# Scan products in sixteen 32x32 tiles and four banks, with the state kept in SBUF and updated by VectorE

## Chip, core and metric

The kernel runs on one core of a Trainium2 chip. The metric is the device time of one execution in microseconds (us), the median of several runs.

## What is computed

One block of a transformer on x of shape (2, 4096, 512), in fp32. Only the scan in its attention part is touched by the change:

```python
k, v = x @ Wk.T, x @ Wv.T                  # 16 heads of 32; k is rotated by position (cos/sin)
W = eye(32) per batch and head             # the state
for each chunk of 16 tokens (256 chunks):
    z    = kc @ W
    grad = kc.T @ ((z - vc) * 2/(16*32))
    W    = W - grad
out = layernorm(z of all chunks) * gamma + beta
x1  = layernorm(x + out @ Wo.T)
y   = down(silu(gate(x1)) * up(x1))        # 512 -> 1408 -> 512, ternary weights with scales
result = layernorm(x1 + y)
```

The chunks depend on one another: 256 steps, each of which reads the state that the step before it left.

## The kernel before

The work goes in ticks. Tick t takes tokens 128t to 128t+127 of both batches, and each tick works on several such tiles of tokens at once, at different depths: it projects k and v of tile t, and of tile t+1 for batch 0 (`project_k`, `project_v`, `rotate`), runs the eight scan steps of tile t-1 (sc), normalises z of tile t-2 and projects it with Wo (`project_o`, `add_o`), and does the feed-forward of tiles t-2 and t-3 (`gate_up`, `down`), of which the last normalisation belongs to tile t-4. A tick has 16 slots (`SLOTS`). Every engine runs its own written-out list of slots, in order, and waits on semaphores; there is no scheduler. What stands in a slot, and in which order inside it, is the order on that engine's queue.

Scan step i takes two slots. In the even slot 2i TensorE makes z (`scan_z`, line 698: 16 fp32 products of 64 columns on tiles of 64x32, each of them two records in the trace), VectorE subtracts v from it (`scan_err`, line 925: four instructions, one for each quarter of the partitions, which leave the other half of every `err` row block at zero), and ScalarE copies z out of PSUM into `v_rows` for storing (`save_z`, line 519). In the odd slot 2i+1 TensorE adds the products of k and err to the state in PSUM (`scan_state`, line 713: 8 products of 128 columns on tiles of 64x32, which accumulate for the whole kernel), and ScalarE copies the state from PSUM to SBUF with the factor -STEP (`keep_state`, `copy_state`, line 510: four instructions), where the next `scan_z` reads it.

Between the scan's products TensorE has full-size work. After the state products of slot 13 it does `down` (line 751, four products) and then the first nine products of `project_v` for batch 0 of the next tile (line 725). These wait for `k_mul`, which VectorE's `rotate` raises (lines 909 and 914), since both projections use the one PSUM bank `work`: rotate reads k from it, and then v may overwrite it. `rotate(t + 1, 0)` is VectorE's first item in slot 13.

```python
dve.wait_ge(k_projected, 2 * n + b + 1)      # rotate: three operations, then k_mul is at 6n + 3b + 3
pe.wait_ge(k_mul, 6 * n + 3 * b + 3)         # project_v
```

In slots 0, 2, 8 and 10 ScalarE's `save_z` stands behind `gate` (line 534), which waits for that slot's `gate_up` on TensorE. Ticks 3 to 30 all have this form (28 of them). In tick 1 and most of tick 2 there is no feed-forward work, and ticks 31 and 32 have no projection of a new tile.

## Time and profile before

| | us |
|---|---|
| median of 3 runs | 2057.38 |
| lowest, highest | 2052.96, 2057.82 |
| the profiled execution | 2071.61 |
| its span, first to last instruction | 2069.7 |
| mean granted TensorE clock in it | 0.965 of full |

The page gives the busy time of every engine; the windows view splits it by stage; the lines view groups instructions by line, with the mean of one and the idle time of the engine just before them; the timeline shows instructions in order of time. "issue" as a releaser is idle time for which the profile shows no wait. PE is TensorE's products, PEld its weight loads, DVE is VectorE, ACT ScalarE, POOL GpSimd.

### The profile page before, as it was taken

Reading aid. Unit: us, or ns where it says so; the run is one execution under the profiler, and the core shown is the slowest. Engines: PE = TensorE matmul, PEld = TensorE weight load, DVE = VectorE, ACT = ScalarE, POOL = GpSimd, SP = SyncE. Lnnn points to the kernel's source line nnn. Section 1 sums busy time; section 2 is a strip of 40 time slices with the busy share of each in tenths; the row PEclk is TensorE's granted clock in tenths of the full one; section 3 lists DMA queues with packets and bytes.
Section 4 is the critical chain, followed back from the end, with each engine's and each line's share of the span. In section 5 each row is a group of like instructions: output and inputs, shape, how many; then the busy total and the mean of one; then the engine's idle time right before and its main releaser. Section 6 shows DMA issues by size and latency. Waiting matters only on the chain.

```text
span 2069.7 us, 53846 instructions
## 1 busy us (share of the span) xinstructions
PE 1869.2 (90%) x21656; PEld 1460.7 (71%) x21656; DVE 1300.4 (63%) x2878; ACT 914.4 (44%) x2258; POOL 641.1 (31%) x778
## 2 busy tenths in 40 slices
PE   3235999999999999999999999999999999999887
PEld 2123777777777777777777777777777777777765
DVE  2247676667666766676666667666676676666642
ACT  1122544444444444444444444444444444444422
POOL 1001233332333333323323333233333333333222
PEclk8677999999999999999999999999999999999999
DMA  5574444454555444544544445445444454444320
GB/s 188 191 221 142 135 143 143 140 153 128 148 157 153 139 137 140 153 132 145 157 150 130 147 141 150 134 145 155 144 140 146 142 149 130 149 146 147 93 78 27
DMA packets 314194, 294.02 MB, mean 142 GB/s; under 512 B 42968, under 2 KB 264408, under 8 KB 313944
## 3 DMA queue, kind: packets, MB, share of 16 engines
q1 hardware_dynamic: 302048, 272.21, 44.2%
q10 hardware_dynamic: 11896, 18.35, 2.7%
q8 instruction: 173, 2.83, 0.6%
q14 instruction: 77, 0.63, 0.1%
HBM read 156.19 MB, written 142.87 MB: 144 GB/s over the span
## 4 chain that ended last, share of the span: by engine, by line
PE 47%; DVE 24%; DMA 11%; issue 7%; SPq 4%; ACT 3%; POOL 2%; ACTq 1%; DVEq 0%; POOLq 0%
PE work L725 18%; PE gu_acc L739 16%; DVE err L925 9%; PE down_acc L751 8%; DMA landed<-zT_scr 5%; DMA zT_scr<-turned 4%; DVE hid L932 3%; DVE turned L864 3%; PE z_acc L698 2%; DVE stats L845 2%; DVE x_tok L859 2%; PE state_acc L713 2%; POOL rstd L431 2%; SPq L307 2%; SPq L261 2%
## 5 line engine op out<-in xcount | busy, mean ns | idle before, releaser
L453 POOL TENSOR_TENSOR hid_lo<-hid,hid_hi 128x256 fp32r<-128x256 f32 x352 | 261.8, 744 | 905.1 <-ACT hid_hi L544 905.1
L925 DVE TENSOR_TENSOR err<-z_acc,v_rows 32x256 f32<-32x256 f32 x1024 | 429.1, 419 | 113.8 <-PE z_acc L698 87.8
L510 ACT ACTIVATE state<-state_acc 32x256 f32<-32x256 f32 x1028 | 384.5, 374 | 76.3 <-PE state_acc L713 57.0
L739 PE MATMUL gu_acc<-x_hi,gw 128*128 128x256 f32 x1408 | 386.3, 307 | 34.0 <-DVE hid L932 30.9
L534 ACT ACTIVATE hid<-gu_acc,gate_scale 128x256 f32<-128x256 f32 x352 | 166.7, 474 | 413.0 <-PE gu_acc L739 412.2
L739 PE MATMUL gu_acc<-x_lo,gw 128*128 128x256 f32 x1408 | 348.1, 280 | 0.0
L739 PE MATMUL gu_acc<-x_hi,uw 128*128 128x256 f32 x1408 | 347.5, 280 | 0.0
L739 PE MATMUL gu_acc<-x_lo,uw 128*128 128x256 f32 x1408 | 346.9, 279 | 0.0
L739 PEld LDWEIGHTS gu_acc<-x_hi,gw 128*128 128x128 f32 x1408 | 265.3, 188 | 98.9 <-DVE hid L932 74.9
L932 DVE SCALAR_TENSOR_TENSOR hid<-gu_acc,up_scale,hid 128x256 f32<-128x256 f32 x352 | 168.8, 479 | 262.2 <-ACT hid L534 258.4
L751 PE MATMUL down_acc<-dw,hid_hi 128*128 128x512 f32 x704 | 281.8, 400 | 1.0 <-POOL hid_lo L453 1.0
L751 PE MATMUL down_acc<-dw,hid_lo 128*128 128x512 f32 x704 | 278.7, 396 | 0.0
L739 PEld LDWEIGHTS gu_acc<-x_lo,gw 128*128 128x128 f32 x1408 | 266.0, 189 | 0.1
L739 PEld LDWEIGHTS gu_acc<-x_hi,uw 128*128 128x128 f32 x1408 | 265.0, 188 | 0.0
L739 PEld LDWEIGHTS gu_acc<-x_lo,uw 128*128 128x128 f32 x1408 | 264.8, 188 | 0.0
L519 ACT ACTIVATE v_rows<-z_acc 128x256 f32<-128x256 f32 x256 | 97.6, 381 | 342.9 <-DVE err L925 342.9
L725 PE MATMUL work<-wv,fm 128*128 128x512 f32 x744 | 196.9, 407 | 56.9 <-DVE k_sin L914 56.9
L544 ACT ACTIVATE hid_hi<-hid 128x256 fp32r<-128x256 f32 x352 | 147.1, 418 | 175.7 <-DVE hid L932 174.8
L725 PE MATMUL work<-wo,fm 128*128 128x512 f32 x768 | 200.2, 411 | 25.9 <-DVE fm L946 24.5
L725 PE MATMUL work<-wk,fm 128*128 128x512 f32 x756 | 201.9, 416 | 10.6 <-DVE fm L956 10.6
L725 PEld LDWEIGHTS work<-wv,fm 128*128 128x128 f32 x744 | 137.8, 192 | 89.9 <-DVE k_sin L914 57.9
L725 PEld LDWEIGHTS work<-wo,fm 128*128 128x128 f32 x768 | 144.2, 194 | 62.1 <-DVE fm L946 28.1
(74 smaller groups left out, 2083.9 us busy)
## 6 DMA issues: line engine op xcount, KB each, us to landing
x_fm<-xT SPq DMA_DIRECT2D x64, 256.0 KB, 3.5
k_scr<-k_tok SPq DMA_DIRECT2D x32, 512.0 KB, 3.9
k_rows<-k_scr SPq DMA_DIRECT2D x512, 32.0 KB, 2.1
v_rows<-v_scr SPq DMA_DIRECT2D x512, 32.0 KB, 2.1
z_scr<-v_rows SPq DMA_DIRECT2D x32, 512.0 KB, 3.2
z_tok<-z_scr SPq DMA_DIRECT2D x512, 32.0 KB, 1.8
x_tok<-x SPq DMA_DIRECT2D x32, 512.0 KB, 3.8
zT_scr<-turned SPq DMA_DIRECT2D x128, 128.0 KB, 3.1
```

The source lines that it names most:

```text
L261: sp.dma_start(place[:, i0:i0 + NS // 2, :], scr[b, i0 * MB:i0 * MB + P // 2, hg * P:(hg + 1) * P] .rearrange("(i t) c -> t i c", t=MB)).t ...
L453: pool.tensor_tensor(hid_lo[m % RING][:], hid[m % 2][:], hid_hi[m % RING][:].bitcast(F32), ALU.subtract).then_inc(hid_lo_ready, 1)
L510: act.activation(state[q, :, e].rearrange("p (r g) e -> p r g e", r=2), state_acc[q, :, 0:P].rearrange("p r (g e) -> p r g e", e=HEAD), AC ...
L519: act.activation(v_rows[:, i].rearrange("p a (r c) -> p a r c", r=2), z_acc[:, :, 0:P].rearrange("p r (a c) -> p a r c", a=2), ACT.Copy).t ...
L534: act.activation(hid[m % 2][:], gu_acc[:, 0:TOK], ACT.Silu, scale=gate_scale[:, m:m + 1]).then_inc(silu_done, 1)
L544: act.activation(hid_hi[m % RING][:], hid[m % 2][:], ACT.Copy).then_inc(hid_hi_ready, 1)
L725: mm = pe.matmul(acc[:], lhsT=fm[p_x][:, c, b, :], rhs=w[p_w][:, c, :], start=(c == 0 and k == 0), stop=(c == NC - 1 and k == 2))
L739: mm = pe.matmul(gu_acc[:, k * TOK:(k + 1) * TOK], lhsT=w[:, c, m * P:(m + 1) * P].bitcast(dt), rhs=part[:, c].bitcast(dt), start=(c == 0 ...
L751: mm = pe.matmul(down_acc[b][:], lhsT=part[m % RING][:, b * P:(b + 1) * P].bitcast(dt), rhs=dw[:, m, :].bitcast(dt), start=(m == 0 and par ...
L864: dve.transpose(turned[:, :, b * NC:(b + 1) * NC, :], src[:, b, :].rearrange("p (c h d) -> p h c d", c=NC, h=HQ)).then_inc(done, 1)
L925: dve.tensor_tensor(err[q, g:g + 2, :, :].rearrange("p a (r h) e -> p a r (h e)", r=2), z_acc[q, :, 0:P].rearrange("p r (a c) -> p a r c", ...
L932: dve.scalar_tensor_tensor(hid[m % 2][:], gu_acc[:, TOK:2 * TOK], up_scale[:, m:m + 1], hid[m % 2][:], ALU.mult, ALU.mult).then_inc(hid_re ...
```

## The change

The four PSUM banks of state and z become one tensor `scan_acc` of four banks. z stays in columns 0 to 127 of banks 2 and 3. The product of k and err no longer accumulates in PSUM: it is 16 products of 64 columns on tiles of 32x32, row tile j into columns 128 to 191 of bank j (`step_acc`). `err` holds no zero halves any more, and is written by one instruction over 128 partitions. The state lives in SBUF; VectorE adds the step to it with two instructions (`step_state`), whose scalar column `half_step` is -STEP on the partitions that belong to the half and 0 on the others. ScalarE's `copy_state` and `keep_state` are gone. `scan_z` no longer waits for `z_saved`; `scan_state` waits for it ahead of row tile 2. The state's starting value is loaded by a DMA and `begin_state` is gone.

```diff
-        err = sb("err", [P, NG // 2, HQ, HEAD])
+        err = sb("err", [P, 2, HQ, HEAD])
+        half_step = sb("half_step", [P, 2])
...
-        state_acc = bank_pair("state_acc")
-        z_acc = bank_pair("z_acc")
+        scan_acc = ctx.enter_context(nc.psum_tensor("scan_acc", [P, NG // 2, 512], F32))
+        z_acc = scan_acc[:, 2:4, 0:P]
+        step_acc = scan_acc[:, :, P:P + 2 * HEAD]
...
-            sp.dma_start(eye_rep, ident_rep.rearrange("p (g e) -> p g e", g=NG)).then_inc(small_in, 16)
+            sp.dma_start(state[:], begin.rearrange("p (g e) -> p g e", g=NG)).then_inc(small_in, 16)
...
             def save_z(n, i):
-                act.wait_ge(err_ready, 4 * NS * n + 4 * i + 4)
+                act.wait_ge(err_ready, NS * n + i + 1)
...
-                    if within(sc) and s % 2 == 1:
-                        keep_state(sc, s // 2)
...
             def scan_z(n, i):
-                pe.wait_ge(state_ready, 4 * NS * n + 4 * i + 4)
                 if i >= 1 or n >= 1:
-                    pe.wait_ge(z_saved, NS * n + i)
+                    pe.wait_ge(state_ready, 2 * (NS * n + i))
...
             def scan_state(n, i):
-                pe.wait_ge(err_ready, 4 * NS * n + 4 * i + 4)
-                for r in range(2):
-                    k = slice(r * P // 2, (r + 1) * P // 2)
+                pe.wait_ge(err_ready, NS * n + i + 1)
+                for j in range(NG // 2):
+                    k = slice(j * HEAD, (j + 1) * HEAD)
+                    if j == 2:
+                        pe.wait_ge(z_saved, NS * n + i + 1)
                     for h in range(HQ):
                         q = slice(h * HEAD, (h + 1) * HEAD)
-                        mm = pe.matmul(state_acc[q, r, 0:P], lhsT=k_rows[k, i, q], rhs=err[k, :, h, :],
-                                       start=False, stop=False, skip_group_check=True,
-                                       tile_position=(r * P // 2, h * HEAD))
-                        if r:
+                        mm = pe.matmul(step_acc[q, j, :], lhsT=k_rows[k, i, q], rhs=err[k, :, h, :], start=True,
+                                       stop=True, skip_group_check=True, tile_position=(j * HEAD, h * HEAD))
+                        if j == NG // 2 - 1:
                             mm.then_inc(state_added, 1)
...
             def scan_err(n, i):
-                for j in range(NG // 2):
-                    q = slice(j * HEAD, (j + 1) * HEAD)
-                    g = j % 2 * 2
-                    dve.wait_ge(z_done, 4 * NS * n + 4 * i + j + 1)
-                    dve.tensor_tensor(err[q, g:g + 2, :, :].rearrange("p a (r h) e -> p a r (h e)", r=2),
-                                      z_acc[q, :, 0:P].rearrange("p r (a c) -> p a r c", a=2),
-                                      v_rows[q, i].rearrange("p a (r c) -> p a r c", r=2),
-                                      ALU.subtract).then_inc(err_ready, 1)
+                dve.wait_ge(z_done, 4 * NS * n + 4 * i + 4)
+                dve.tensor_tensor(err[:].rearrange("p a (r h) e -> p a r (h e)", r=2),
+                                  z_acc.rearrange("p r (a c) -> p a r c", a=2),
+                                  v_rows[:, i].rearrange("p a (r c) -> p a r c", r=2),
+                                  ALU.subtract).then_inc(err_ready, 1)
+
+            def step_state(n, i):
+
+                dve.wait_ge(state_added, 4 * NS * n + 4 * i + 4)
+                for e in range(2):
+                    part = state[:, :, e * HEAD:(e + 1) * HEAD].rearrange("p (j o) e -> p j o e", o=2)
+                    dve.scalar_tensor_tensor(part, step_acc.rearrange("p j (o e) -> p j o e", o=2),
+                                             half_step[:, e:e + 1], part, ALU.mult, ALU.add).then_inc(state_ready, 1)
...
                 for s in range(SLOTS):
+                    if within(sc) and s % 2 == 1:
+                        step_state(sc, s // 2)
                     if within(o) and s in (7, 8):
                         add_o(o, s - 7)
```

On VectorE's queue, slots 12 to 14 of a steady tick stood so before (`x_lo` is the low part of x1, `x_tok<-down_acc` the scaling of the feed-forward's output):

```order
L925 TENSOR_TENSOR err<-z_acc,v_rows 32x256 [waits z_done] x4
L961 TENSOR_TENSOR x_lo<-landed,x_hi 128x4x128 [waits x1_hi_ready]
L909 TENSOR_TENSOR k_tok<-work,rot 128x512 [waits k_turned,k_stored,v_stored,rot_in0,k_projected]
L914 TENSOR_TENSOR k_sin<-work,rot 128x16x16 x2
L961 TENSOR_TENSOR x_lo<-landed,x_hi 128x4x128 [waits x1_hi_ready]
L942 TENSOR_TENSOR x_tok<-down_acc,down_scale 128x512 [waits down_done,x1_ready]
```

and now so (line numbers are those of the changed file):

```order
L890 TENSOR_TENSOR err<-scan_acc,v_rows 128x256 [waits z_done]
L934 TENSOR_TENSOR x_lo<-landed,x_hi 128x4x128 [waits x1_hi_ready]
L900 SCALAR_TENSOR_TENSOR state<-scan_acc,half_step,state 128x8x32 [waits state_added]
L900 SCALAR_TENSOR_TENSOR state<-scan_acc,half_step,state 128x8x32
L877 TENSOR_TENSOR k_tok<-work,rot 128x512 [waits k_turned,k_stored,v_stored,rot_in0,k_projected]
L882 TENSOR_TENSOR k_sin<-work,rot 128x16x16 x2
L934 TENSOR_TENSOR x_lo<-landed,x_hi 128x4x128 [waits x1_hi_ready]
```

Four instructions have become one, and two new ones, which wait for TensorE's `state_added`, stand ahead of the three of `rotate`.

On TensorE's queue, slot 13 and the start of slot 14 stood so before:

```order
L713 MATMUL state_acc<-err,k_rows 32x128 [waits err_ready]
L713 MATMUL state_acc<-err,k_rows 32x128 x7
L751 MATMUL down_acc<-dw,hid_hi 128x512 [waits hid_lo_ready]
L751 MATMUL down_acc<-dw,hid_lo 128x512
L751 MATMUL down_acc<-dw,hid_hi 128x512
L751 MATMUL down_acc<-dw,hid_lo 128x512
L725 MATMUL work<-wv,fm 128x512 [waits k_mul]
L725 MATMUL work<-wv,fm 128x512 x8
L698 MATMUL z_acc<-state,k_cols 32x64 [waits z_saved,state_ready]
```

and now so:

```order
L684 MATMUL scan_acc<-err,k_rows 32x64 [waits err_ready]
L684 MATMUL scan_acc<-err,k_rows 32x64 x7
L684 MATMUL scan_acc<-err,k_rows 32x64 [waits z_saved]
L684 MATMUL scan_acc<-err,k_rows 32x64 x7
L721 MATMUL down_acc<-dw,hid_hi 128x512 [waits hid_lo_ready]
L721 MATMUL down_acc<-dw,hid_lo 128x512
L721 MATMUL down_acc<-dw,hid_hi 128x512
L721 MATMUL down_acc<-dw,hid_lo 128x512
L695 MATMUL work<-wv,fm 128x512 [waits k_mul]
L695 MATMUL work<-wv,fm 128x512 x8
L667 MATMUL scan_acc<-state,k_cols 32x64 [waits state_ready]
```

The order is the same, with eight more products in the state block and a second wait in its middle; the nine products of `project_v` still wait for `k_mul`.

## Rows read from the trace of the kernel before

**Rows 1.** Page, part 1: busy time (share of the span) and instructions.
```profile
PE 1869.2 (90%) x21656; PEld 1460.7 (71%) x21656; DVE 1300.4 (63%) x2878; ACT 914.4 (44%) x2258; POOL 641.1 (31%) x778
```

**Rows 2.** Windows: stretch, length, busy of PE, PEld, DVE, ACT, POOL, clock, DMA.
```profile
89.75:208.00 118.25, 59.15 (x887) 38.20 (x887) 68.17 (x123) 35.71 (x89) 11.73 (x15) 0.74 0.64 191
208.00:1900.00 1692.00, 1647.55 (x19376) 1293.50 (x19376) 1135.62 (x2545) 808.23 (x2007) 568.93 (x686) 1.00 0.49 144
1900.00:1980.00 80.00, 67.84 (x876) 53.78 (x875) 49.19 (x112) 38.05 (x97) 24.29 (x31) 0.96 0.33 98
```

**Rows 3.** Page, part 5: busy, mean ns of one, idle before.
```profile
L925 DVE TENSOR_TENSOR err<-z_acc,v_rows 32x256 f32<-32x256 f32 x1024 | 429.1, 419 | 113.8 <-PE z_acc L698 87.8
L510 ACT ACTIVATE state<-state_acc 32x256 f32<-32x256 f32 x1028 | 384.5, 374 | 76.3 <-PE state_acc L713 57.0
L932 DVE SCALAR_TENSOR_TENSOR hid<-gu_acc,up_scale,hid 128x256 f32<-128x256 f32 x352 | 168.8, 479 | 262.2 <-ACT hid L534 258.4
```

**Rows 4.** Timeline, slot 13 of tick 16: start, duration, engine, [idle before it].
```profile
1026.32 0.69 DVE L909 TENSOR_TENSOR k_tok<-work,rot 128x512 f32<-128x512 f32 x1
1026.63 0.18 PEld L713 LDWEIGHTS state_acc<-err,k_rows 64*32 64x32 f32 x16 [0.36 <-issue]
...
1026.93 0.74 DVE L914 TENSOR_TENSOR k_sin<-work,rot 128x256 f32<-128x256 f32 x2
...
1027.01 0.50 PE L751 MATMUL down_acc<-dw,hid_hi 128*128 128x512 f32 x1
...
1027.26 1.58 ACT L510 ACTIVATE state<-state_acc 32x256 f32<-32x256 f32 x4 [1.18 <-PE state_acc L713]
...
1028.04 2.26 PE L725 MATMUL work<-wv,fm 128*128 128x512 f32 x9
```

**Rows 5.** Timeline, the z block of slot 12, same tick.
```profile
1022.32 0.29 PEld L698 LDWEIGHTS z_acc<-state,k_cols 64*32 64x32 f32 x32 [0.36 <-issue]
...
1022.70 2.63 PEld L725 LDWEIGHTS work<-wk,fm 128*128 128x128 f32 x12
```

**Rows 6.** Lines by form, TensorE's two scan blocks.
```profile
L698 PE MATMUL z_acc<-state,k_cols 64*32 64x64 f32 x8192 | 118.5, 225 | 20.0 <-ACT state L510 20.0
L713 PE MATMUL state_acc<-err,k_rows 64*32 64x128 f32 x4096 | 116.6, 285 | 42.0 <-DVE err L925 42.0
```

**Rows 7.** Timeline, slot 8 of the same tick: ScalarE's save of z, then TensorE.
```profile
1010.75 0.38 ACT L519 ACTIVATE v_rows<-z_acc 128x256 f32<-128x256 f32 x1
...
1011.20 0.45 PE L713 MATMUL state_acc<-err,k_rows 64*32 64x128 f32 x16
```

**Rows 8.** Timeline, project_o after a wait, in two ticks; the clock after the first.
```profile
764.26 4.61 PE L725 MATMUL work<-wo,fm 128*128 128x512 f32 x12 [1.97 <-DVE fm L946]
...
1060.12 3.07 PE L725 MATMUL work<-wo,fm 128*128 128x512 f32 x12 [2.38 <-DVE fm L946]
...
764.30:769.00 4.70, 4.70 (x28) 3.31 (x28) 3.94 (x9) 1.00 (x3) 0.73 (x1) 0.64 0.12 42
```

**Rows 9.** Waits: engine, line, waited for, us in total, times, longest.
```profile
PEld gu_acc L739 <- DVE hid L932: 74.9, 173, 1.8
```

**Rows 10.** Timeline of ticks 1 and 2, before the feed-forward has started.
```profile
107.30 1.77 DVE L925 TENSOR_TENSOR err<-z_acc,v_rows 32x256 f32<-32x256 f32 x4 [4.77 <-PE z_acc L698]
...
109.13 0.45 PE L713 MATMUL state_acc<-err,k_rows 64*32 64x128 f32 x16 [1.90 <-DVE err L925]
...
111.44 0.68 PE L698 MATMUL z_acc<-state,k_cols 64*32 64x64 f32 x32 [1.85 <-ACT state L510]
...
149.87 1.29 DVE L845 BATCH_NORM_STATS2 stats<-z_tok 128x6 f32<-128x512 f32 x2 [13.51 <-DMA z_tok<-z_scr]
```

**Rows 11.** Timeline of ticks 31 and 32: first, longest and last scan waits.
```profile
1912.48 0.45 PE L713 MATMUL state_acc<-err,k_rows 64*32 64x128 f32 x16 [0.78 <-DVE err L925]
...
1929.45 0.46 PE L698 MATMUL z_acc<-state,k_cols 64*32 64x64 f32 x32 [2.05 <-ACT state L510]
...
1972.67 0.46 PE L698 MATMUL z_acc<-state,k_cols 64*32 64x64 f32 x32 [1.33 <-ACT state L510]
```

More of the change, by code:

```diff
@@ L39 @@
 HALF_UNITS = {1: (0, 2), 2: (2, NC)}
+ZEROED = 3
+SMALL = 8
 LN_EPS = 1e-5
@@ L46, in within, with build @@
     return 0 <= n < NT
-def build(nc, xT, x, wkT, wvT, woT, gamma, beta, gwT, uwT, dwT, gs, us, ds_row, rope, ident, ident_rep, out):
+def build(nc, xT, x, wkT, wvT, woT, gamma, beta, gwT, uwT, dwT, gs, us, ds_row, rope, ident, begin, halves, out):
     with ExitStack() as ctx:
@@ L266, in load_k_half0 @@
                 sp.wait_ge(k_stored, 16 * (n + 1))
-                if n == 0:
-                    sp.wait_ge(state_begun, 2 * HQ)
-                else:
+                if n >= 1:
                     sp.wait_ge(state_added, 4 * NS * (n - 1) + 2 * NS)
@@ L423, in _ @@
         def _(pool):
-            for buf in (v_rows, k_cols, err, state):
+            for buf in (v_rows, k_cols):
                 pool.memset(buf[:], 0.0).then_inc(zeroed, 1)
             pool.memset(neg_half[:], -0.5).then_inc(zeroed, 1)
-            pool.wait_ge(zeroed, 5)
+            pool.wait_ge(zeroed, ZEROED)
             def inverse_root(norm, n):
@@ L504, in _ @@
         def _(act):
-            def copy_state():
-                for h in range(HQ):
-                    q = slice(h * HEAD, (h + 1) * HEAD)
-                    e = slice(h % 2 * HEAD, (h % 2 + 1) * HEAD)
-                    act.activation(state[q, :, e].rearrange("p (r g) e -> p r g e", r=2),
-                                   state_acc[q, :, 0:P].rearrange("p r (g e) -> p r g e", e=HEAD),
-                                   ACT.Copy, scale=-STEP).then_inc(state_ready, 1)
             def high_part(w, stage, c):
@@ L666, in _ @@
         def _(pe):
-            def begin_state():
-                pe.wait_ge(small_in, 16 * 7)
-                pe.wait_ge(zeroed, 5)
-                for r in range(2):
-                    for h in range(HQ):
-                        q = slice(h * HEAD, (h + 1) * HEAD)
-                        pe.matmul(state_acc[q, r, 0:P], lhsT=eye[:, q],
-                                  rhs=eye_rep[:, r * NG // 2:(r + 1) * NG // 2, :], start=True, stop=False,
-                                  skip_group_check=True, tile_position=(0, h * HEAD)).then_inc(state_begun, 1)
             def find_bias():
@@ L689, in scan_z @@
                     pe.wait_ge(k_cols_ready, 4 * n + (2 if i == 0 else 4))
-                pe.wait_ge(state_ready, 4 * NS * n + 4 * i + 4)
                 if i >= 1 or n >= 1:
-                    pe.wait_ge(z_saved, NS * n + i)
+                    pe.wait_ge(state_ready, 2 * (NS * n + i))
+                else:
+                    pe.wait_ge(small_in, 16 * SMALL)
                 for odd in range(2):
@@ L798, in tick @@
                         gate_up(f1, EARLY_GU[s], ffn_dt)
-                    if t == 0 and s == 0:
-                        begin_state()
                     if within(t) and t >= EARLY_TICKS and s == 1:
@@ L1074 @@
     eye = np.eye(P, dtype=np.float32)
-    eye_rep = np.zeros((P, NG, HEAD), np.float32)
+    begin = np.zeros((P, NG, 2 * HEAD), np.float32)
+    halves = np.zeros((P, 2), np.float32)
     for p in range(P):
-        eye_rep[p, :, p % HEAD] = -1.0 / STEP
+        begin[p, :, p % (2 * HEAD)] = 1.0
+        halves[p, p // HEAD % 2] = -STEP
     arrays = {
@@ L1084 @@
         "ds_row": np.broadcast_to(np.asarray(L0_ffn_down_s), (P, DM)),
-        "rope": rope_table(), "ident": eye, "ident_rep": eye_rep.reshape(P, NG * HEAD),
+        "rope": rope_table(), "ident": eye, "begin": begin.reshape(P, NG * 2 * HEAD),
+        "halves": halves,
     }
```

23 lines of the change are left out of this document (6 added, 17 removed).

## The prediction

> **What bounds the kernel.** I read the page's busy times first: TensorE has products under way for 90% of the span, VectorE 63%, ScalarE 44% [rows 1]. A share over the whole span mixes stages, so the windows come next [rows 2]. From 208 to 1900 us TensorE is busy 1647.6 of 1692 us at full clock, so there the order on its queue is the time. From 89.75 to 208 us it is busy for half of 118 us, at 0.74 of its clock, and at the end, 1900 to 1980, for 67.8 of 80 us. In those two stretches something else ends the waits, and the scan is a candidate.
>
> In the steady ticks the scan's own waits are nearly absent: TensorE waited 42.0 us for `err` and 20.0 us for the state copy in the whole run [rows 6], and the timeline puts most of that before 208 and after 1900. The scan chain is hidden behind `gate_up`, `down` and the projections. So making it shorter is worth nothing there, and what counts is whether the change makes TensorE wait in a place where it does not wait now.
>
> **Part by part, against the profiled execution's 2071.6 us.**
>
> *ScalarE* loses 1028 copies of 374 ns, 384.5 us [rows 3]. In the steady ticks nobody waits for them, so this is worth about nothing.
>
> *VectorE.* Before, `err` was 1024 instructions of 419 ns, 429 us [rows 3]. The length of an instruction goes with the elements of a partition, not with the number of partitions, so one over 128 partitions also takes some 0.42 us: 256 of them are 107 us, 322 us less. Added are 512 instructions of 256 elements, of the same kind as the scaling of hid, 479 ns [rows 3]: +245 us. VectorE becomes emptier, by 77 us, but its queue gets a new kind of wait: in each odd slot it now stands still until TensorE has done that slot's state block.
>
> *Slot 13, the term that decides.* In tick 16 `rotate` starts at 1026.32 and is done at 1027.67, while TensorE does its state block and four products of `down`; TensorE then starts `project_v` at 1028.04 without a wait [rows 4]. The slack is under 0.4 us. In the new order the two state updates stand in front of `rotate`. They cannot start before the state block is done, and the row that shows when that is seen by another engine is ScalarE's copy, which had waited 1.18 us for it and starts at 1027.26 [rows 4]. On VectorE the next instruction starts some 0.08 us before the one ahead has ended (1026.32 + 0.69 against 1026.93), so the pair takes 2 x 0.40 = 0.80 us from `rotate`'s view: it starts at 1028.06 and ends at 1029.41 instead of 1027.67. TensorE's first product moves from 1028.04 to about 1029.45, and the first product after a pause is 0.1 us longer (0.50 against 0.40) [rows 4]: 1.5 us. Behind the waiting VectorE stand low_x1 and the scaling of y, both needed only later; behind the waiting TensorE stands the whole tick, and no later wait in the tick is on anything that is not started from this same queue, so the 1.5 us are not given back. Ticks 3 to 30 are 28 ticks: **+42 us**. Ends: a pair of 0.70 to 0.96 us gives 1.4 to 1.7 us, +39 to +47.
>
> *The clock after such a stall.* The steady trace has six waits of 1.57 to 2.38 us ahead of `project_o`. After three of them the granted clock fell (0.64 in the 4.7 us behind the first, so for a part of it at the 1.2 GHz level) and the twelve products took up to 4.61 us instead of 3.07; after the other three, the longest among them, it did not [rows 8]. The new stall is at the short end and has four full products between it and the state block. I take one tick in four: 7 x 1.5 = **+10 us**; ends 0 and 28 x 1.5 = +42.
>
> *The state block itself.* Before, 16 records of 128 columns on 8 tiles; now 32 records of 64 columns on 16 tiles. The nearest row is the z block, 32 records of 64 columns on 8 tiles. From its first weight load to the next full-size one it takes 0.38 us (1022.32 to 1022.70) [rows 5], and the state block takes the same 0.38 (1026.63 to 1027.01), both after 0.36 us of "issue" [rows 4, 5]. Busy time per block is equal too, 118.5/256 and 116.6/256 us [rows 6]. So: **0**. Ends: 0.08 us less a block, since a record is 225 instead of 285 ns [rows 6] (-20 us in 256 blocks), and 0.04 more (+10).
>
> The second wait, for `z_saved`, could stop the block in its middle. In slots 0, 2, 8 and 10 the save stands behind `gate`; in slot 8 it ran from 1010.75 to 1011.13, and the block starts at 1011.20 [rows 7]. It just fits, and the other slots have more room: 0, within the +10.
>
> By the Trainium skill, TensorE: Matmul & The Clock Gate, section Measured speedup vs the span model, a packed group takes one product's duration plus some 4 ns for each further one. With a record of 225 ns and 31 more that is 0.35 us of busy time against 0.46, or an estimated 28 us less in 256 blocks, and a total near 2061; the z block, also 32 records, does not follow it, with 0.46.
>
> *Waits for hid.* TensorE's weight loads waited 74.9 us in 173 cases for the scaling of hid [rows 9], part of it because VectorE was at `err` or ScalarE at a save or copy. With `err` 1.3 us shorter I take 0.25 us a tick: **-7 us**; ends 0 and -12.
>
> *The start.* In tick 1 a step is limited by the chain: 1.77 us of `err`, 1.90 us waited by the state products, 1.85 us waited by the next z [rows 10]. The new chain is shorter by 1.35 us in `err` and 0.7 us in the copy (1.58 against 0.88), less some 0.4 us for the save of z, about 1.6 us a step where no projection stands between. That holds in about half of tick 1's eight steps. But then VectorE waits 13.5 us for a DMA that brings z_tok [rows 10], in a stretch where the DMA queues carry 191 GB/s [rows 2]; this wait starts earlier, and need not end as much earlier. In tick 2 VectorE itself is the busy one (68.2 of 118 us), and z of the second step has to wait for a state update that stands behind that DMA wait. I take **-8 us**, ends 0 and -14. The setup that goes (`begin_state` and a first copy) is covered by transfers. Tick 2 also has the stall of slot 13: **+1**.
>
> *The end.* Ticks 31 and 32 have six scan waits of 0.78 to 2.05 us [rows 11], 8.2 us together, and no `rotate`. The shorter chain takes most: **-6 us**, ends 0 and -8.
>
> Sum: +42 + 10 + 0 - 7 - 8 + 1 - 6 = **+32 us**, 2103.6 against the profiled 2071.6. The median of the runs is 14.2 us (0.7%) below that execution, so I put the difference on it: 2057.4 + 32 = **2089 us**. With the middling ends of the terms this case runs from 2064 to 2112.
>
> **Rivals.**
>
> *A. The clock falls at most of the stalls.* Same stall, but its cost is 3.0 instead of 1.5 us in nearly every tick. For it: three of six waits of this length did so. Against: the longest did not, and dense work stands around the new one. +32 + 32 = 2121 us. Chance 0.10.
>
> *B. Faster: the state block is cheaper.* Place: the eight state blocks of a tick. If sixteen tiles really work side by side, the block shrinks to one weight load and its drain, some 0.2 of 0.38 us, and 256 blocks give back 46 us: 2089 - 46 = 2043 us. It decides from 0.13 us a block, where the 32 us are paid back; above it the kernel gets faster. Against: the z block has the same count of records and shows no such thing. Chance 0.08.
>
> *C. The small gains cancel the stall.* No change of clock, 0.04 us less a block (-10), start -14, end -8, hid -12: 43 - 44 = -1, or 2056 us. Each end is possible, all together are not likely. Chance 0.07.
>
> The forecast case, slower with a clock that falls now and then, has 0.75. About 0.3% is what a measurement of this kernel can tell from no change. Slower is the forecast and A, 0.85; the same is C, 0.07; faster is B, 0.08. The range 2062 to 2118 takes in the forecast's ends and part of A, and leaves out B, C and the rest of A.
>
> **What would show it.** Right, if the changed profile has: TensorE waiting some 28 times about 1.4 us ahead of `project_v` (first nine products), released by the k_sin instructions of `rotate`; in each such tick `rotate` directly behind two state updates of 0.4 to 0.5 us; `err` at 256 x 0.42 us; ScalarE's busy time down by 384 us without effect; steady ticks some 1.5 us longer; and 0.38 us from the state block's first weight load to the next full-size one. Wrong, if `project_v` follows `down` without a wait, if the state block is under 0.25 us or over 0.5, if TensorE waits in the middle of it for `z_saved`, or if the clock row shows falls in most ticks. The largest doubt is the clock; the next the start, where DMA and scan take turns.

## The result and the profile after

| | before | after |
|---|---|---|
| median of 6 runs each, same chip, us | 2055.45 | 2068.68 |
| lowest, highest | 2049.06, 2058.63 | 2064.87, 2071.99 |
| the profiled execution | 2071.61 | 2071.99 |
| its span | 2069.7 | 2070.0 |
| mean granted TensorE clock in it | 0.965 | 0.969 |

The ratio is 1.0066, 95% interval 1.0047 to 1.0085: 13 us slower. The direction and the range held; of the 32 us forecast, 13 came. The two profiled executions are equally long, so their difference is not the change's price: the one of before lies some 16 us above the median in the table, the one of after 3 us. They serve to see each part.

Page of the changed kernel, part 1:

```profile
PE 1865.3 (90%) x25736; PEld 1479.9 (71%) x25736; DVE 1176.0 (57%) x2622; ACT 543.8 (26%) x1230; POOL 647.0 (31%) x776
```

Its lines by form (busy, mean ns of one, idle before):

```profile
L900 DVE SCALAR_TENSOR_TENSOR state<-scan_acc,half_step,state 128x256 f32<-128x256 f32 x512 | 223.1, 476 | 221.3 <-PE scan_acc L684 217.3
L890 DVE TENSOR_TENSOR err<-scan_acc,v_rows 128x256 f32<-128x256 f32 x256 | 107.4, 419 | 113.0 <-PE scan_acc L667 101.3 <-DMA v_rows<-v_scr 11.5
L684 PE MATMUL scan_acc<-err,k_rows 32*32 32x64 f32 x8192 | 104.5, 228 | 18.2 <-DVE err L890 18.0
```

`err` over 128 partitions takes the 419 ns that it took over 32 [rows 3], the updates 476 ns. ScalarE lost 371 us of 914 [rows 1], for which TensorE had waited 20.0 us [rows 6], at start and end.

Timeline of slot 13 of tick 16 after, which answers to [rows 4]:

```profile
1028.27 0.23 PEld L684 LDWEIGHTS scan_acc<-err,k_rows 32*32 32x32 f32 x32 [0.37 <-issue]
...
1028.59 0.19 PEld L721 LDWEIGHTS down_acc<-dw,hid_hi 128*128 128x128 f32 x1
...
1028.93 0.88 DVE L900 SCALAR_TENSOR_TENSOR state<-scan_acc,half_step,state 128x256 f32<-128x256 f32 x2 [2.21 <-PE scan_acc L684]
...
1029.72 0.68 DVE L877 TENSOR_TENSOR k_tok<-work,rot 128x512 f32<-128x512 f32 x1
1030.32 0.74 DVE L882 TENSOR_TENSOR k_sin<-work,rot 128x256 f32<-128x256 f32 x2
...
1031.12 2.36 PE L695 MATMUL work<-wv,fm 128*128 128x512 f32 x9 [1.33 <-DVE k_sin L882]
```

VectorE waited 2.21 us for the state block, did both updates, then `rotate`; TensorE stood 1.33 us. Two more things can be read: the state block now takes 0.32 us from its first weight load to the next full-size one (1028.27 to 1028.59), not 0.38, and no wait stands in its middle (in the whole run 1.1 us in 5 cases).

Waits of the whole run after (engine, line, waited for: us in total, times, longest):

```profile
PE work L695 <- DVE k_sin L882: 96.6, 31, 54.5
...
PE scan_acc L667 <- DVE state L900: 18.4, 9, 7.1
PE scan_acc L684 <- DVE err L890: 18.0, 9, 6.3
PE work L695 <- DVE fm L919: 10.4, 11, 3.4
...
PEld gu_acc L709 <- DVE hid L905: 46.0, 77, 1.8
```

Before, the first of these was 56.9 us in 3 cases: 28 stalls have come, as forecast. But two others shrank. The weight loads' waits for hid went from 74.9 in 173 cases [rows 9] to 46.0 in 77; most of that was hidden behind products under way, for the products' own waits for hid went only from 30.9 to 26.6. And the waits of TensorE for `fm`, ahead of `project_o`, went from 24.5 us in 25 cases to 10.4 in 11, of which the steady ticks hold 2.3 us in 6; the three falls of the clock behind such waits [rows 8] are gone as well. The windows of after (compare [rows 2]) show the clock at full in the steady part, where three short falls were too little to show in before's 1.00, and at the end, where before had 0.96:

```profile
89.75:208.00 118.25, 68.24 (x1189) 46.82 (x1189) 61.37 (x110) 15.93 (x33) 13.31 (x17) 0.74 0.64 193
208.00:1900.00 1692.00, 1631.13 (x22867) 1300.13 (x22866) 1019.81 (x2303) 473.53 (x1080) 573.16 (x682) 1.00 0.48 144
1900.00:1980.00 80.00, 71.25 (x1148) 57.25 (x1148) 46.80 (x112) 22.66 (x53) 25.55 (x33) 1.00 0.35 107
```

### The profile page after: what moved, and what is told of

It reads as the page before. It is cut to its first block, busy times and chain, and to the rows that moved or that the text cites. A ratio compares the mean times of both kernels' runs of the same rounds, so it can differ in the third digit from the quotient of the medians.

```text
span 2070.0 us, 60526 instructions
## 1 busy us (share of the span) xinstructions
PE 1865.3 (90%) x25736; PEld 1479.9 (71%) x25736; DVE 1176.0 (57%) x2622; ACT 543.8 (26%) x1230; POOL 647.0 (31%) x776
## 4 chain that ended last, share of the span: by engine, by line
PE 71%; DVE 10%; DMA 6%; issue 6%; ACT 2%; SPq 2%; ACTq 1%; POOL 1%; DVEq 0%; POOLq 0%
PE gu_acc L709 30%; PE work L695 24%; PE down_acc L721 10%; PE scan_acc L684 4%; PE scan_acc L667 4%; DMA landed<-zT_scr 3%; DVE turned L832 3%; DVE state L900 2%; DMA zT_scr<-turned 2%; DVE hid L905 2%; ACT hid L518 1%; ACTq L567 1%; DVE k_sin L882 1%; DVE x_tok L827 1%; SPq L304 1%
## 5 line engine op out<-in xcount | busy, mean ns | idle before, releaser
L709 PE MATMUL gu_acc<-x_hi,gw 128*128 128x256 f32 x1408 | 388.4, 309 | 29.6 <-DVE hid L905 26.6
L709 PE MATMUL gu_acc<-x_hi,uw 128*128 128x256 f32 x1408 | 353.1, 283 | 0.0
L709 PE MATMUL gu_acc<-x_lo,uw 128*128 128x256 f32 x1408 | 351.7, 281 | 0.0
L900 DVE SCALAR_TENSOR_TENSOR state<-scan_acc,half_step,state 128x256 f32<-128x256 f32 x512 | 223.1, 476 | 221.3 <-PE scan_acc L684 217.3
L695 PE MATMUL work<-wo,fm 128*128 128x512 f32 x768 | 198.4, 408 | 12.9 <-DVE fm L919 10.4
L507 ACT ACTIVATE v_rows<-scan_acc 128x256 f32<-128x256 f32 x256 | 97.6, 381 | 358.1 <-DVE err L890 358.1
L695 PEld LDWEIGHTS work<-wk,fm 128*128 128x128 f32 x756 | 141.3, 194 | 46.0 <-DVE fm L929 10.1
```

Source lines behind the costliest of these rows:

```text
L507: act.activation(v_rows[:, i].rearrange("p a (r c) -> p a r c", r=2), z_acc.rearrange("p r (a c) -> p a r c", a=2), ACT.Copy).then_inc(z_s ...
L695: mm = pe.matmul(acc[:], lhsT=fm[p_x][:, c, b, :], rhs=w[p_w][:, c, :], start=(c == 0 and k == 0), stop=(c == NC - 1 and k == 2))
L709: mm = pe.matmul(gu_acc[:, k * TOK:(k + 1) * TOK], lhsT=w[:, c, m * P:(m + 1) * P].bitcast(dt), rhs=part[:, c].bitcast(dt), start=(c == 0 ...
L900: dve.scalar_tensor_tensor(part, step_acc.rearrange("p j (o e) -> p j o e", o=2), half_step[:, e:e + 1], part, ALU.mult, ALU.add).then_inc ...
```

## How the runs are compared

Twelve runs were made in three batches, each on one chip, with the kernel before beside them: "ratio" is the time over that of the kernel before in the same batch. That kernel had medians of 2055 to 2063 us; the changed one had 2068.68 and 2067.27. So a difference between two kernels of different batches is told by ratios and by medians, and where the two disagree by some us, both stand.

From TensorE's timeline I split each profiled execution at the twelve products of `project_v` in slot 4: "start" is the time of the first in tick 3, "tick" the mean of the 28 distances up to tick 31, "shortest" the least of them, "end" the rest of the span. "po" are TensorE's waits of over 0.15 us ahead of `project_o` between 230 and 1840 us, their sum and their number, "falls" the `project_o` in there that took over 4 us for twelve products instead of 3.06.

```
kernel                  ratio   median   start  tick   shortest  end    po        falls
before                  1       2055-63  226.7  59.06  58.03     189.2  20.8, 23  3
after                   1.0066  2068.7   220.5  59.49  59.33     183.7   2.3,  6  0
after again             1.0057  2067.3   212.5  59.52  59.27     185.0   3.8,  7  0
rotate first            0.9802  2022.2   215.1  58.00  57.67     184.3   5.1, 13  0
 + turn later           0.9751  2006.8   214.2  57.39  57.08     184.7   3.8,  7  0
 + err in four          1.0057  2074.4   226.7  59.05  57.93     190.9  17.9, 23  1
err in four             1.0265  2116.9   228.8  60.56  59.53     191.4  14.0, 17  2
 + old tiles            1.0275  2121.9   228.2  60.81  59.91     193.1  13.3, 13  1
four but in step 7      1.0250  2110.6   231.7  60.42  59.49     191.7  12.4, 14  1
four in step 0 alone    1.0104  2085.2   217.3  60.22  59.27     183.5  19.4, 21  2
four but in step 0      1.0217  2108.7   225.4  60.33  59.56     194.4  11.6, 16  1
late save in step 7     1.0060  2069.3   216.5  59.50  59.26     184.8   2.9,  8  0
before + stall          1.0227  2110.9   229.7  60.46  59.68     186.0  16.2, 19  1
before + wait alone     1.0101  2081.7   225.8  59.55  58.76     186.4  16.8, 16  1
```

## The experiments

**1. What the stall is worth: rotate ahead of the state updates.**

```diff
                 for s in range(SLOTS):
+                    if within(t + 1) and s == 13:
+                        rotate(t + 1, 0)
                     if within(sc) and s % 2 == 1:
                         step_state(sc, s // 2)
...
-                    if within(t + 1) and s == 13:
-                        rotate(t + 1, 0)
```

> The changed kernel with one edit: in slot 13 VectorE does rotate(t + 1, 0) before the two state updates instead of behind them. Theory S (the stall ahead of project_v costs its full 1.4 us in each of 28 ticks and nothing gives it back): the 1.33 us waits ahead of project_v are gone and the kernel is about 40 us faster than the changed one, near 2029 us, ratio to the kernel before 0.987. Theory G (a large part of the stall is given back by later waits of the same tick, so it was worth only some 13 us net): near 2055 us, ratio 1.00, with new waits in other places, ahead of project_o above all.

2022.17 us, ratio 0.9802 (0.9776 to 0.9828). Against the changed kernel that is 45 to 47 us by medians, 52 to 54 by ratios; the shortest tick fell from 59.27 or 59.33 to 57.67, so a stall costs 1.6 us of a tick, and 28 of them 45 (the mean tick fell by 1.5, which makes 42). Timeline of VectorE and TensorE in slot 13 of this run:

```profile
1003.04 0.69 DVE L877 TENSOR_TENSOR k_tok<-work,rot 128x512 f32<-128x512 f32 x1 [0.73 <-PE work L695]
1003.65 0.75 DVE L882 TENSOR_TENSOR k_sin<-work,rot 128x256 f32<-128x256 f32 x2
...
1004.52 0.88 DVE L900 SCALAR_TENSOR_TENSOR state<-scan_acc,half_step,state 128x256 f32<-128x256 f32 x2
...
1005.22 1.09 PE L695 MATMUL work<-wv,fm 128*128 128x512 f32 x4
```

`project_v` follows without a wait. The kernel is faster than both: without the stall the rest of the change gains some 2% on the kernel before. The forecast gave the rest 21 us, so something it holds is worth about twice that.

**2. The stall put into the kernel before.** Two more operations on VectorE of the size of the state updates, behind the same wait, ahead of `rotate` in slot 13; all else as before. They write to a part of `k_tok` that is rewritten later.

```diff
+                    if within(sc) and within(t + 1) and s == 13:
+                        dve.wait_ge(state_added, 4 * NS * sc + 4 * (s // 2) + 4)
+                        dve.wait_ge(k_stored, 16 * (t + 1))
+                        dve.wait_ge(k_turned, 2 * (t + 1))
+                        for half in range(2):
+                            dve.scalar_tensor_tensor(k_tok[:, 1, half * 256:(half + 1) * 256], down_scale[:, 0:256],
+                                                     neg_half[:, 0:1], down_scale[:, 256:512],
+                                                     ALU.mult, ALU.add)
```

> The kernel before, with only this added ahead of rotate in slot 13: VectorE waits for the state products of that slot and then does two operations of 256 elements into a part of k_tok that nobody reads any more. Nothing of the change is in it, only its stall. Theory S (the stall costs its full length): waits of 1.3 us ahead of project_v in ticks 1 to 30 and +38 to +44 us, 2094 to 2100 us, ratio 1.02. Theory G (the tick gives a part back by itself, without the shorter err): under +25 us, and shorter waits ahead of project_o than in the kernel before.

2110.93 us, ratio 1.0227 (1.0196 to 1.0258): +47 us, a little above what was expected: the shortest tick is 1.65 us longer, which makes 46 in 28. The stall has about the same price in either kernel, and by these times nothing of it is given back. (The mean tick is only 1.40 us longer than in the profile of before, whose execution was a long one, with more waits ahead of `project_o`.)

**3. The wait alone.** The first wait of experiment 2, without the operations.

```diff
+                    if within(sc) and within(t + 1) and s == 13:
+                        dve.wait_ge(state_added, 4 * NS * sc + 4 * (s // 2) + 4)
```

> The kernel before, where VectorE in slot 13 waits for the state block ahead of rotate, without any added work. By the rows of before rotate then starts near 1027.2 instead of 1026.3 us in tick 16, of which under 0.4 us is slack. If slack and wait are sized rightly: 0.6 us a tick, project_v released by k_sin in 28 ticks with waits of 0.4 to 0.6 us, +14 to +20 us on the kernel before. If the wait were the whole stall: +40 or more. If the slack were larger: 0 to +5.

2081.66 us, ratio 1.0101 (1.0082 to 1.012): +21 us. Timeline of one tick:

```profile
1031.41 0.69 DVE L909 TENSOR_TENSOR k_tok<-work,rot 128x512 f32<-128x512 f32 x1 [0.97 <-PE state_acc L713]
...
1032.82 2.37 PE L725 MATMUL work<-wv,fm 128*128 128x512 f32 x9 [0.46 <-DVE k_sin L914]
```

The wait on TensorE is 0.46 us and the shortest tick is 0.73 longer; 28 x 0.73 = 20. The slack was as small as [rows 4] said. Of the 1.6 us of a stall somewhat under half is VectorE standing at the state block, the rest the two updates.

**4. err in four again, in the changed kernel.** The stall stays.

```diff
-                dve.wait_ge(z_done, 4 * NS * n + 4 * i + 4)
-                dve.tensor_tensor(err[:].rearrange("p a (r h) e -> p a r (h e)", r=2),
+                for j in range(NG // 2):
+                    q = slice(j * HEAD, (j + 1) * HEAD)
+                    dve.wait_ge(z_done, 4 * NS * n + 4 * i + j + 1)
+                    dve.tensor_tensor(err[q].rearrange("p a (r h) e -> p a r (h e)", r=2),
```

> The changed kernel with err made by four instructions again, one for each quarter of the partitions, as before the change. Theory Q (with the shorter err the save of z in slot 14 is earlier, the store and loads that SyncE's queue holds behind it are earlier, and so the transfer of the normalised z is on time: this is where the waits ahead of project_o went): these waits come back, 10 us or more together, and the kernel is 10 to 25 us slower than the changed one, 2079 to 2093 us. Theory N (they vary from run to run by themselves, and err is hidden everywhere but at start and end): 2 to 8 us slower, from the start and the end alone, 2071 to 2077 us.

2116.92 us, ratio 1.0265 (1.0236 to 1.0294): 41 to 43 us above the changed kernel by ratios, 48 to 50 by medians, more than either theory had. The single instruction is worth that much, where the forecast's three terms that hold it (hid, start, end) make 21. The table says where: the start is 8 to 16 us longer, the end 6 to 8, the mean tick 1.05 longer (29 us in 28), of which only 0.2 is in the shortest tick. Waits ahead of `project_o` are back (14.0 us), with two falls of the clock. Laid over the changed kernel tick by tick, TensorE's timeline loses 0.5 to 0.6 us of the 1.05 at the first `project_o` of a tick (the wait and the slower products), 0.2 ahead of the second, and the rest, some 0.3, at the start of `gate_up` blocks. These last two are spread over all ticks and are not in the column "po".

**5. The old tiles on top.** Two rows of 64x32 tiles with 128 columns instead of four of 32x32 with 64, zero halves in `err`, and the wait for `z_saved` ahead of the block; still without accumulating.

```diff
-                for j in range(NG // 2):
-                    k = slice(j * HEAD, (j + 1) * HEAD)
-                    if j == 2:
-                        pe.wait_ge(z_saved, NS * n + i + 1)
+                pe.wait_ge(z_saved, NS * n + i + 1)
+                for r in range(2):
+                    k = slice(r * P // 2, (r + 1) * P // 2)
```

> As the run with four err instructions, and the products of k and err again 8 on tiles of 64x32 with 128 columns, into two banks, err with its zero halves; the state still lives in SBUF and VectorE updates it. It differs from that run by the shape of the tiles. Theory P (sixteen tiles of 32x32 make the state block 0.05 us shorter, 0.33 against 0.38 us from its first weight load to the next full-size one): 0.38 us again, and 8 x 0.05 us a tick, 10 to 13 us slower than the run with four err instructions. Theory Z (no difference in length, as was forecast): within 3 us of it. Here the whole block waits for the save of z; if that shows as a wait, it is on top.

2121.88 us, ratio 1.0275 (1.0247 to 1.0304): 2 to 5 us above experiment 4, whose interval it overlaps, so the time decides between neither theory. In the profile the shortest tick is 0.38 us longer, and the block is as before:

```profile
1023.83 0.18 PEld L683 LDWEIGHTS scan_acc<-err,k_rows 64*32 64x32 f32 x16 [0.36 <-issue]
1024.21 0.19 PEld L709 LDWEIGHTS gu_acc<-x_hi,gw 128*128 128x128 f32 x1 [0.20 <-issue]
```

0.38 us against 0.32 to 0.33 with 32x32 tiles. Eight blocks of a tick make 0.4 us, 11 us in 28 ticks, as the shortest tick has it; by medians only 5 of it can be seen. The length of the block is shown, its price in the run is not.

**6. Both together: rotate first, err in four.**

> rotate ahead of the state updates, and err in four instructions: what is left of the change is the state in SBUF, VectorE's updates and the 32x32 tiles. If the parts add, it is 43 us above the run with rotate first alone (2022 us beside 2061.5 of before), 2065 us, so within 8 us of the kernel before on either side. If the four instructions cost more where there is no stall ahead to hide the late chain: 2070 to 2080.

2074.38 us, ratio 1.0057 (1.0037 to 1.0077). With experiments 1 and 4 and the changed kernel this fills a square of medians:

```
                     rotate first   rotate behind the updates
err in one           2022.2         2067.3, 2068.7
err in four          2074.4         2116.9
```

By medians the stall costs 42 to 47 us in either row, the four instructions 48 to 52 in either column, so the parts add. By ratios the stall costs 52 to 54 with one instruction and 43 with four, a difference no larger than what the four intervals allow together. It also says what remains: the state in SBUF with VectorE's updates and new tiles is 12 us slower than the kernel before, where I had it at nothing. In the profile its end is 190.9 us, against 186.0 and 186.4 in the two variants of the kernel before of experiments 2 and 3 (189.2 in the profile of before itself), and its mean tick 59.05, against 60.46 - 1.6 = 58.86 and 59.55 - 0.73 = 58.82 there. By that estimate some 5 us are lost at the end and 5 to 6 in the ticks; against the profile of before itself, a long execution, it would be 2 us and nothing. Where the 12 us lie, and why the ticks are not shorter in spite of the cheaper block, was not tried and stays open.

**7. Is it the save of z?** After the profiles of experiments 1, 2, 4 and 5 I held that the short `err` brings the save of step 7 and with it z's way out and back ahead. Four small copies on ScalarE ahead of that save:

```diff
+                if i == NS - 1:
+                    for c in range(4):
+                        act.activation(late[:, c], z_acc[:, c // 2, c % 2 * 2 * HEAD:(c % 2 + 1) * 2 * HEAD], ACT.Copy)
```

> The changed kernel, with four small copies on ScalarE ahead of the save of z in step 7 alone, so that the save ends some 1 us later; VectorE and TensorE have the same instructions. Theory K (the short err moves the chain save of z, store, reload, turn, store ahead, and that is why project_o hardly waits any more): waits ahead of project_o come back, 10 to 20 us in the steady ticks, with a fall of the clock now and then, and the run is 8 to 20 us longer than the changed kernel. Theory V (it is VectorE's lighter queue that took those waits away): nothing changes, within 4 us of the changed kernel.

2069.32 us, ratio 1.006 (1.0042 to 1.0078), and beside it the changed kernel again:

> The changed kernel again, beside the others of this batch. Both theories: ratio to the kernel before 1.0066 with 1.005 to 1.009, some 2068 to 2075 us; ticks of 59.3 us when undisturbed, waits ahead of project_o in the steady ticks under 5 us together and no fall of the clock.

2067.27 us, ratio 1.0057 (1.0039 to 1.0075). Nothing changed, so the run speaks against theory K, but weakly: the copies took less than I had planned,

```profile
1031.07 0.57 ACT L510 ACTIVATE late<-scan_acc 128x64 f32<-128x64 f32 x4 [8.02 <-DVE err L894]
1031.49 0.42 ACT L511 ACTIVATE v_rows<-scan_acc 128x256 f32<-128x256 f32 x1
```

and the store of z was only 0.47 us later.

**8. One instruction in step 7 alone,** four in the others.

> err in four instructions in steps 0 to 6, in one in step 7. The run with four everywhere was 41 us above the changed kernel; its profile had 14 us of waits ahead of project_o in the steady ticks and two falls of the clock. Theory K: the waits go again (under 6 us in the steady ticks), and of the 41 us some 15 to 20 come back: 20 to 27 us above the changed kernel, start and end being as long as with four. Theory V: seven eighths of VectorE's added load stay, so the waits stay too: 34 to 41 us above.

2110.61 us, ratio 1.025 (1.0228 to 1.0271), 43 us above the changed kernel in this batch (40 by ratios); 12.4 us of waits ahead of `project_o`. Theory K falls: a short `err` in step 7 is not enough to take those waits away.

**9 and 10. The other end of the chain: step 0.** SyncE's queue in tick 17 after the change (issues; the last of tick 16's z, then the output, v, x and z's turned copy), and what VectorE does at its place:

```profile
1034.94 0.34 SPq L242 DMA_DIRECT2D z_scr<-v_rows  x1
1036.67 0.77 SPq L251 DMA_DIRECT2D z_tok<-z_scr  x2
1037.48 3.71 SPq L260 DMA_DIRECT2D k_rows<-k_scr  x8
1042.30 0.40 SPq L375 DMA_DIRECT2D out<-x_tok  x1
1042.73 4.17 SPq L260 DMA_DIRECT2D v_rows<-v_scr  x8
...
1054.97 0.34 SPq L330 DMA_DIRECT2D landed<-zT_scr  x1
```

```profile
1040.84 0.42 DVE L890 TENSOR_TENSOR err<-scan_acc,v_rows 128x256 f32<-128x256 f32 x1 [0.57 <-PE scan_acc L667]
1041.18 1.09 DVE L827 TENSOR_SCALAR x_tok<-x_tok,moments,rstd 128x512 f32<-128x512 f32 x2
```

`err` of step 0, the normalisation of y behind it (done at 1042.27), the store of the output at 1042.30: SyncE stood from 1041.19 for it. Behind it stand the eight loads of v and, some 13 us on, the reload of z's turned copy (`landed`). `fm` is made from that, and `project_o` waits for `fm`. Two variants, four instructions in step 0 alone and in all but step 0:

```diff
+                for j in range(NG // 2 if i == 0 else 1):
+                    q = slice(j * HEAD, (j + 1) * HEAD) if i == 0 else slice(0, P)
```

> err in four instructions in step 0 alone, in one in the other seven. The profiles show a chain that begins at the err of slot 0: the normalisation of y behind it on VectorE starts 1.2 us later with four (both in the kernel before and in the two runs with four in step 0), so do the store of the output and the eight loads of v that SyncE issues after it, and the landing of z's turned copy (issue of its reload 0.8 us after the start of project_v with one instruction, 1.7 to 2.1 with four). Theory F (this chain makes project_o wait): waits ahead of project_o of 10 us or more in the steady ticks, the reload at 1.7 to 2.1 us, and 15 to 25 us above the changed kernel. Theory L (it is VectorE's load as a whole): one eighth of the added load, at most 6 us above.

> err in one instruction in step 0, in four in the other seven. Theory F: waits ahead of project_o stay under 6 us in the steady ticks, the reload near 0.8 us, steady ticks of 59.5 to 59.7 us; what is left is the longer chain at start and end, so 15 to 25 us above the changed kernel. Theory L: as with four everywhere, 38 to 45 us above.

With four in step 0 alone, the same places:

```profile
1039.49 0.78 SPq L251 DMA_DIRECT2D z_tok<-z_scr  x2
1040.31 3.71 SPq L260 DMA_DIRECT2D k_rows<-k_scr  x8
1046.37 0.39 SPq L375 DMA_DIRECT2D out<-x_tok  x1
```

```profile
1043.53 1.78 DVE L892 TENSOR_TENSOR err<-scan_acc,v_rows 32x256 f32<-32x256 f32 x4 [0.44 <-PE scan_acc L667]
1045.34 1.00 DVE L827 TENSOR_SCALAR x_tok<-x_tok,moments,rstd 128x512 f32<-128x512 f32 x2
```

SyncE is ready at 1044.02 and stands for 2.35 us. The waits ahead of `project_o` are back in full, 19.4 us in 21 cases of the steady ticks, with two falls of the clock, while start (217.3) and end (183.5) stay short. In the whole run they are, against the 10.4 us in 11 cases above:

```profile
PE work L695 <- DVE fm L921: 27.6, 26, 4.0
```

The mean tick is 0.73 us longer, and the timeline has all of that at the first `project_o`. One eighth of VectorE's added load brought all of these waits, so they come from the chain from step 0, as theory F has it, and not from the load as a whole. The price: 2085.24 us, ratio 1.0104 (1.0084 to 1.0124); 17 to 18 us above the changed kernel by medians, 8 to 10 by ratios, so below or at the low end of the expected 15 to 25.

With four in all but step 0, theory F's half failed: 2108.67 us, ratio 1.0217 (1.0197 to 1.0236), 31 to 33 us above by ratios, 40 to 41 by medians, and 11.6 us of waits ahead of `project_o`. SyncE's queue shows a reason:

```profile
1053.25 0.34 SPq L242 DMA_DIRECT2D z_scr<-v_rows  x1
1054.97 0.77 SPq L251 DMA_DIRECT2D z_tok<-z_scr  x2
1055.79 3.71 SPq L260 DMA_DIRECT2D k_rows<-k_scr  x8
1059.54 0.43 SPq L375 DMA_DIRECT2D out<-x_tok  x1
```

Here the output's store follows the loads of k at once; y has been ready, and it is the queue that is late, since the save of step 7 came 1.2 us later. Two chains meet at this store: the queue from the save of step 7, and y from the `err` of step 0. Measured from the start of `project_v` in slot 4, the medians over the 28 ticks are:

```
                         store of z   store of out   reload of z's turned copy
one in all (after again) -19.09       -11.73          0.81
late save in step 7      -18.62       -11.48          1.19
four in step 0 alone     -19.09       -10.49          2.15
four but in step 0       -17.88       -10.83          1.86
four but in step 7       -19.13       -10.52          1.71
four in all              -17.92       -10.53          1.96
before                   -17.90       -10.53          2.07
```

Only where both chains are early is the store near -11.7 and the reload near 0.8. That would be why experiment 8 could not free the waits, and neither could this one. It was read from these queues after the fact: a run with four instructions in steps 1 to 6 alone, which leaves both chains early, would test it and was not made. Theory L is not refuted for the rest of the price either: at the first `project_o` a tick of this run loses 0.3 us, but another 0.4 to 0.5 us ahead of the second one and of `gate_up`, which experiment 9 does not lose. In the changed kernel the landing just suffices: `project_o` is wanted at 6.74, and waits in 6 or 7 ticks of 28.

**11. One more wait taken away.** With rotate first, the second transposition of x1 in slot 9 behind the scaling of hid, which `gate_up` of slot 10 waits for.

```diff
                         turn_x1(o, 0)
-                        turn_x1(o, 1)
...
                         scale_hid(f2, LATE_GU[s])
+                    if within(o) and s == 9:
+                        turn_x1(o, 1)
```

> The kernel with rotate ahead of the state updates (2022 us), and the second transposition of x1 in slot 9 moved behind the scaling of hid, for which gate_up of slot 10 waits 0.65 us in every tick. If that wait is due to the transposition alone: 28 x 0.65 = 18 us less, 2004 us. If the next link is nearly as late (the store and reload of x1 start later by one instruction, or the scaling waits for ScalarE then): 0 to 10 us less, 2012 to 2022.

2006.78 us, ratio 0.9751 (0.973 to 0.9773), 15 us below experiment 1 by medians (10 by ratios) and 49 below the kernel before. The shortest tick is 0.59 us shorter, and the waits of TensorE's weight loads for hid fall from 45.9 us to:

```profile
PEld gu_acc L709 <- DVE hid L905: 27.4, 75, 1.8
```

This is the best version found.

## Why the prediction held in sign and missed in size

*Slot 13.* Right in place, count and mechanism. 28 stalls of 1.33 us on TensorE make ticks 1.5 to 1.6 us longer: 42 to 45 us, for a forecast of 42. Experiments 1 to 3 price it in both kernels, and its two halves. "No later wait in the tick is on anything that is not started from this same queue, so the 1.5 us are not given back" held too: put into the kernel before, the stall cost 47 us.

*The step that failed* is another: "The scan chain is hidden behind `gate_up`, `down` and the projections. So making it shorter is worth nothing there." On that ground the shorter `err` got -7 us in the steady ticks, for waits for hid, and TensorE's waits ahead of `project_o` got no term at all. Experiment 4 measured 1.05 us of each tick, 29 us in 28. Of these, 0.5 to 0.6 us (some 15 us in 28 ticks) stand at the first `project_o`, whose waits went from 20.8 to 2.3 us with the change. The waits were there to be read [rows 8]; I used these rows only to price the clock behind a new stall, and did not follow them back. They hang on a transfer that stands on SyncE's queue behind the store of the output, and this waits for work that stands behind an `err` on VectorE. Experiment 9 shows that link: four instructions in step 0 alone bring all of these waits back. The short `err` moved that store by 1.2 us. The other half of the 29 us lies ahead of the second `project_o` and of `gate_up`, and no experiment takes it apart. The rows were also miscounted: of waits of 1.57 us and more there are seven, not six, and the clock fell behind three of the seven.

*The clock after the stall.* The second step that failed: +10 forecast, none measured. 28 stalls of 1.33 us, each with four full products between it and the state block, left the clock at 1.00 from 208 to 1980 us (the windows above). The falls that there were before sat behind waits ahead of `project_o`, and the change removed these.

*The start and the end.* Forecast -8 and -6. The start (212.5 to 220.5 in three profiles, against 226.7 in that of before) came out 6 to 14 us shorter, up to the end of its range; the end 4 to 6, as forecast (183.7 to 185.0 against 189.2), though only 1 to 3 against the variants of the kernel before. With hid the three terms that hold the short `err` made 21 us; experiments 4 and 6 measured 48 to 52 by medians, 41 to 43 by ratios. What was missing is mostly in the steady ticks.

*The state block.* Forecast 0, with the z block as nearest row. It was 0.05 us shorter, 0.4 us a tick: a count of 32 records alone does not set it, since the z block with 32 records on 64x32 tiles takes 0.38 and this one on 32x32 tiles 0.32 to 0.33. Rival B needed 0.13 us to decide and did not come near it. The span model of the Trainium skill (TensorE: Matmul & The Clock Gate, Measured speedup vs the span model) would have 0.35 us of busy time, by an estimate that counts each of the 32 records as a tile; the row has 0.41 (104.5/256 us), between it and the z block's 0.46 [rows 6].

*The move of the state to VectorE.* Costed at nothing in the steady ticks and as a gain of 0.7 us a step at start and end. Experiment 6 has it, with the cheaper block, at 12 us slower. Part of that may be at the end, where VectorE now does `err` and updates in a row that two engines had shared; this was not shown.

*The sum.* Against the forecast of 32 us, the clock took nothing instead of 10, the short `err` gave 49 instead of 21, the stall cost 45 instead of 43, and the rest cost 12 instead of nothing: +8 us by medians, for a measured 13. That it comes near proves little, since the terms come from one square of runs, whose sides close by themselves. It is in part luck that the time fell inside the range: two misses of 10 and 28 us on one side met one of 12 on the other. Of the signs that were named, the 28 waits, `err` at 0.42 us and the clock without falls were right or better than right; the block of 0.38 us and ticks longer by some 1.5 us were not (the mean tick grew by 0.43). Rival C, small gains that cancel the stall, was nearer in kind than in its parts: its gain in the ticks, 12 us for hid at most, was 29.

## What to carry to other kernels

A wait that shows in only a few ticks of a steady trace deserves to be followed back to its first link before a change is costed: here a 1.3 us shorter piece of work on an engine with slack was worth 49 us, 29 of them in ticks where it seemed hidden, and about half of these because it stood ahead of a store behind which a whole DMA queue waited. When two operations on one engine are added ahead of a third, ask which of the three the bottleneck engine wants first; writing `rotate` first turned 13 us slower into 2% faster. Where two chains meet at one store, shortening either alone gives little (experiments 8 and 10 are 6 and 8 us below experiment 4), and experiments on one of them mislead.

## What was not expected

- Waits of 1.3 us ahead of `project_v`, 28 in a row, left the granted clock at 1.00; after waits of 1.7 to 2.4 us ahead of `project_o` it fell in one to three ticks of each kernel that had them, to 0.66 in the 5 us behind one of 2.30 us in experiment 10 (4.35 us for twelve products). Length alone does not tell which: the longest, 2.81 us in experiment 5, left it at 1.00.
- A block of 32 records of 64 columns took 0.32 to 0.33 us on sixteen 32x32 tiles, 0.38 on eight 64x32 tiles, and 16 records of 128 columns on those eight took 0.38 too.
- The kernel before, its variants and those with `err` in four in most steps have ticks that differ by 3.4 to 4.3 us in one execution; in the changed kernel, and in the variants with one instruction everywhere, they differ by 0.6 to 1.5. With four in step 0 alone it is 3.7 again.
